# Products of the low-rank remainders with B, two tiles at a time in 64 rows of the array each

## What is computed

```python
x = x + L0(x)   # per head: causal convolution over the 512 positions with a filter K, plus x * D, then a mask by length
x = x + L1(x)   # per sequence b:
    result   = x[b] @ base_weight.T + base_bias          # 32 x 512 by 512 x 512
    h        = x[b] @ lora_A[adapter_ids[b]].T           # rank 16
    lora_out = h @ lora_B[adapter_ids[b]].T              # 16 -> 512
    return result + lora_out
```

## Time and profile before

| | us |
|---|---|
| median of 3 runs (lowest, highest) | 211.22 (211.07, 211.51) |
| the profiled execution | 210.73 |
| its span, first to last instruction | 208.8 |
| PE busy | 190.5 |
| DVE busy | 167.6 |
| ACT busy | 121.8 |
| POOL busy | 89.7 |

### The profile page before, as it was taken

One profiled execution on the slowest core, in us unless ns is written; L12 is line 12 of the kernel. 1 busy time (PEld: TensorE's weight loads), 2 busy tenths in 40 slices (PEclk: granted clock), 3 DMA queues, 4 the chain that ended last, 5 costly groups with the idle time before them and its releaser, 6 DMA issues.

```text
span 208.8 us, 4393 instructions
## 1 busy us (share of the span) xinstructions
PE 190.5 (91%) x1063; PEld 166.3 (80%) x1063; DVE 167.6 (80%) x366; ACT 121.8 (58%) x356; POOL 89.7 (43%) x144
## 2 busy tenths in 40 slices
PE   0049899999999999899999999999999999999993
PEld 0037899999999899788888888888888888888883
DVE  3985698789699976877999978788888878888662
ACT  2798865343636445337767656657566665756530
POOL 4850000001545778085563645546454464544500
PEclk9999999999999999999999999999999999999999
DMA  5984999999999999984877767657676677665334
GB/s 150 365 334 110 359 406 409 410 413 407 409 412 408 408 407 420 347 256 116 262 235 241 223 202 234 208 201 223 210 226 204 220 222 203 232 191 180 101 100 154
DMA packets 21521, 56.47 MB, mean 270 GB/s; under 512 B 3266, under 2 KB 3970, under 8 KB 21250
## 3 DMA queue, kind: packets, MB, share of 16 engines
q1 hardware_dynamic: 18146, 47.68, 62.3%
q0 software_dynamic: 2560, 8.39, 14.0%
q10 hardware_dynamic: 800, 0.23, 0.5%
HBM read 45.64 MB, written 10.65 MB: 270 GB/s over the span
## 4 chain that ended last, share of the span: by engine, by line
PE 82%; DMA 9%; DVE 5%; POOL 1%; issue 1%; SPq 0%; ACT 0%; DVEq 0%; ACTq 0%
PE z_ps L923 25%; PE y_ps L962 20%; PE k_ps L962 20%; DMA strip<-k_pad 7%; PE z_ps L950 7%; PE y_ps L989 2%; PE y_ps L988 2%; PE k_ps L989 2%; PE k_ps L988 2%; DMA par<-params 1%; DMA k_pad<-k_sb 1%; PE y_ps L1011 1%; PE k_ps L1011 1%; PE y_ps L972 1%; PE k_ps L904 1%
## 5 line engine op out<-in xcount | busy, mean ns | idle before, releaser
L923 PE MATMUL z_ps<-xp,strip 128*128 128x512 f32 (+3 forms) x384 | 63.6, 326 | 0.7 <-DMA strip<-k_pad 0.7
L923 PEld LDWEIGHTS z_ps<-xp,strip 128*128 128x128 f32 x384 | 59.3, 196 | 5.0 <-DMA strip<-k_pad 1.2
L410 POOL DMA_INDIRECT b_hl<-b_tab,b_idx x32 | 38.0, 1186 | 15.6 <-issue 9.0
L405 POOL CAST ag<-a_hl 128x128 fp32r x64 | 23.0, 361 | 40.7 <-PE z_ps L950 26.6
L962 PE MATMUL y_ps<-w_hi,xp 128*128 128x512 f32 x120 | 39.5, 390 | 0.0
L962 PE MATMUL k_ps<-w_hi,xp 128*128 128x512 f32 x120 | 39.5, 390 | 0.0
L543 ACT ACTIVATE ag<-a_hl 128x64 fp32r x128 | 25.6, 248 | 20.5 <-issue 20.3
L455 ACT ACTIVATE xp<-z_all 128x512 fp32r<-128x512 f32 x32 | 20.0, 629 | 21.4 <-PE z_ps L923 19.9
L736 DVE TENSOR_TENSOR xp<-z_all,xp 128x512 fp32r<-128x512 f32 x32 | 26.3, 823 | 5.3 <-ACT xp L455 5.2
L962 PEld LDWEIGHTS y_ps<-w_hi,xp 128*128 128x128 f32 x120 | 22.5, 188 | 4.3
L962 PEld LDWEIGHTS k_ps<-w_hi,xp 128*128 128x128 f32 x120 | 22.5, 188 | 4.3
(11 more groups left out here) (137 smaller groups left out, 237.9 us busy)
## 6 DMA issues: line engine op xcount, KB each, us to landing
strip<-k_pad SPq DMA_DIRECT2D x31, 512.0 KB, 7.8
z_all<-x_conv SPq DMA_DIRECT2D x16, 512.0 KB, 8.3
x_t<-x_tile SPq DMA_DIRECT2D x32, 256.0 KB
out<-a_raw SPq DMA_DIRECT2D x31, 256.0 KB
a_raw<-a_t SPq DMA_DIRECT2D x2, 512.0 KB, 7.6
x_t<-b_rows SPq DMA_DIRECT2D x2, 512.0 KB, 8.7
w_sb<-w_t SPq DMA_DIRECT2D x2, 512.0 KB, 9.9
b_tab<-b_hl SPq DMA_DIRECT2D x1, 1024.0 KB, 10.0
```

Source lines behind the costliest of these rows:

```text
L405: last = g.tensor_copy(ag[:, s, :, :, q, :].rearrange("p c e r -> p e c r"), src)
L410: g.indirect_dma_start(out=b_hl[:, t % BS, :].bitcast(F32), out_offset=None, in_=b_tab, in_offset=bass.IndirectOffsetOnAxis(ap=b_idx[:, t: ...
L923: last = nc.tensor.matmul(z_ps[:, h % ZS, m * P:L], strip[:, h % SS, m * P:(m + 1) * P, t], xp[:, h % XS, 0:LC - m, e, :], start=(n == 0), ...
```

## The change

The remainder of h no longer has zeros beside it. Tiles are paired (0 with 1, 2 with 3, up to 28 with 29). The even tile's h_lo lies in partitions 0 to 63 of a buffer, the odd tile's in 64 to 127 of the same buffer. For odd tiles the index table exchanges the halves of B, so that the high part of B lies in partitions 64 to 127 (`b_idx`, `table`). `tile_b` issues the h_hi product for each tile, and after that of the odd tile the two h_lo products of the pair, each over 64 rows, into two banks. A new semaphore `hhi_used` tells ACT that the h_hi product is done. `y_done` of both tiles comes after the odd tile, so DVE evicts both in the even step (`evict`), and none in the odd one. Tile 30 keeps a product over 128 rows, as does tile 31 in its halves; POOL zeroes the other half of their `h_lo` late (`lo_zeroed`), and no longer at the start.

```diff
+        def lo_half(t, s):
+
+            last = isinstance(t, int) and t == NT - 1
+            o = s % 2 * BR
+            return slice(o, o + BR), (s // 2 + last) % TS
...
-            link(g.memset(h_lo[BR:P, :, :].bitcast(F32), 0.0))
...
-            pool.wait_ge(idx_ready, 1)
+            pool.wait_ge(idx_ready, 2)
...
+            pool.wait_ge(gathered, NT)
+            pool.wait_ge(y_done, NT - 4)
+            g.memset(h_lo[BR:P, 1, :].bitcast(F32), 0.0).then_inc(lo_zeroed, 1)
+            pool.wait_ge(lo_zeroed, 1)
+            pool.wait_ge(y_done, NT - 2)
+            g.memset(h_lo[0:BR, 0, :].bitcast(F32), 0.0).then_inc(lo_zeroed, 1)
...
             def h_rounded(t, b, first):
                 act.wait_ge(hm_done, t + 1)
                 if not first:
-                    act.wait_ge(y_done, t + (1 - TS))
+                    act.wait_ge(hhi_used, t + (1 - TS))
...
-                V.tensor_scalar(b_idx[:, :], ids[:, NB:NB + NT], float(R), row_c, ALU.mult,
-                                ALU.add).then_inc(idx_ready, 1)
+                for o in range(2):
+                    V.tensor_scalar(b_idx[:, o::2], ids[:, NB + o:NB + NT:2], float(R), tab[:, NL + 2 + o:NL + 3 + o],
+                                    ALU.mult, ALU.add).then_inc(idx_ready, 1)
...
-            def h_remainder(t, b):
+            def h_remainder(t, s):
+
+                b, (rows, pair) = s % TS, lo_half(t, s)
                 dve.wait_ge(hhi_done, 2 * t + 2)
-                V.tensor_tensor(h_lo[0:BR, b, :], h_m[:, b, :], h_hi[0:BR, b, :].bitcast(F32),
+                V.tensor_tensor(h_lo[rows, pair, :], h_m[:, b, :], h_hi[0:BR, b, :].bitcast(F32),
                                 ALU.subtract).then_inc(hlo_done, 1)
+
+            def evict(i, s, lap, ago):
+
+                dve.wait_ge(y_done, i + (1 - ago))
+                if not isinstance(i, int) or i - ago >= OS:
+                    dve.wait_ge(stored[(s - ago) % OS], 16 * (lap + (s - ago) // OS))
+                V.tensor_tensor(o_sb[:, (s - ago) % OS, :], y_bank(s - ago), bias_sb[:, :], ALU.add).then_inc(o_done, 1)
...
+                elif known and i == NT - 1:
+                    evict(i, s, lap, 1)
+                elif s % 2 == 0 and there(i - 1):
+                    evict(i, s, lap, 2)
+                    evict(i, s, lap, 1)
...
-                nc.tensor.matmul(y_bank(s), h_hi[:, b, :], b_hl[:, s % BS, :], start=False, stop=False)
-                nc.tensor.matmul(y_bank(s), h_lo[:, b, :], b_hl[:, s % BS, :],
-                                 start=False, stop=True).then_inc(y_done, 1)
+                nc.tensor.matmul(y_bank(s), h_hi[:, b, :], b_hl[:, s % BS, :],
+                                 start=False, stop=False).then_inc(hhi_used, 1)
+                if isinstance(t, int) and t == NT - 2:
+                    pe.wait_ge(lo_zeroed, 1)
+                    nc.tensor.matmul(y_bank(s), h_lo[:, lo_half(t, s)[1], :], b_hl[:, s % BS, :],
+                                     start=False, stop=True).then_inc(y_done, 1)
+                elif s % 2:
+                    for q in (s - 1, s):
+                        rows, pair = lo_half(q, q)
+                        nc.tensor.matmul(y_bank(q), h_lo[rows, pair, :], b_hl[rows, q % BS, :],
+                                         start=False, stop=True).then_inc(y_done, 1)
...
+    table[:, NL + 3] = AD * R * (1 - np.arange(P) // BR) + np.arange(P) % R
```

More of the change, by code:

```diff
@@ L105, in build @@
         par = sb("par", [P, 7, NH])
-        tab = sb("tab", [P, NL + 3])
+        tab = sb("tab", [P, NL + 4])
         dt = sb("dt", [P, NH])
@@ L211, in build @@
         base_done, y_done, o_done = sem("base_done"), sem("y_done"), sem("o_done")
+        hhi_used, lo_zeroed = sem("hhi_used"), sem("lo_zeroed")
+        def lo_half(t, s):
+            last = isinstance(t, int) and t == NT - 1
+            o = s % 2 * BR
+            return slice(o, o + BR), (s // 2 + last) % TS
         def in_chunks(a):
@@ L715, in adapter_ids @@
                 dve.wait_ge(ids_in, 16)
-                row_c = tab[:, NL + 2:NL + 3]
                 link(V.tensor_copy(id_f[:, 1, :], ids[:, :]))
@@ L817, in step @@
                     h_masked(i + 1, (s + 1) % TS)
[L818 to L833, removed]
-                                        ALU.add).then_inc(o_done, 1)
+                if known and i == 2:
+                    dve.wait_ge(tab_lo_stored, 16)
+                    dve.wait_ge(bias_in, 16)
+                if known and i == NT:
+                    dve.wait_ge(stored[OS - 1], 16 * (NT // OS - 1))
+                    for n in range(2):
+                        cols = slice(n * L // 2, (n + 1) * L // 2)
+                        dve.wait_ge(y_done, NT + n)
+                        V.tensor_tensor(o_sb[:, OS - 1, cols], y_bank(YS - 1 + n)[:, 0:L // 2], bias_sb[:, cols],
+                                        ALU.add).then_inc(o_done, 1)
+                elif known and i == NT - 1:
[3 more added lines that the diff above has]
+                    evict(i, s, lap, 1)
                 if there(i + 4):
@@ L841, in step @@
                 if there(i + 1):
-                    h_remainder(i + 1, (s + 1) % TS)
+                    h_remainder(i + 1, s + 1)
             def part_of_x1(t, h0, h1, done):
@@ L1018, in last_b @@
                 pe.wait_ge(hlo_done, NT)
+                pe.wait_ge(lo_zeroed, 2)
                 nc.tensor.matmul(y, h_hi[:, b, :], b_hl[:, BS - 1, cols], start=False, stop=False)
-                nc.tensor.matmul(y, h_lo[:, b, :], b_hl[:, BS - 1, cols], start=False, stop=True).then_inc(y_done, 1)
+                nc.tensor.matmul(y, h_lo[:, lo_half(NT - 1, NT - 1)[1], :], b_hl[:, BS - 1, cols], start=False, stop=True).then_inc(y_done, 1)
             for t in range(NT - OS, NT - 2):
@@ L1050 @@
                        np.broadcast_to(g["L0_cond_log_dt"][None, :], (P, NH))], axis=1)
-    table = np.zeros((P, NL + 3), np.float32)
+    table = np.zeros((P, NL + 4), np.float32)
     table[:, 0:NL] = np.concatenate([NC * np.arange(NA), np.arange(NC)])
```

## The result

The kernel after takes 225.44 us (median of 4, 224.06 to 226.81), the kernel before, timed beside it, 211.14 (210.75 to 211.51). The ratio is 1.068 with a 95% interval of 1.0656 to 1.0705: slower. The sign was forecast, the size was not: 214.9 us, with a range to 218.3. The profiled execution took 224.98 us with a span of 222.9, from its first to its last instruction; before it was 210.73 and 208.8.

A forecast was written before the change was run, and what follows sets the result against it. The prediction took PE's stream of matmuls to bound the tile stage. The profiled 210.73 us plus 3.7 for shape changes, with 0 for the other engines, gave 214.4, and 0.49 to the median made 214.9; range 209.0 to 218.3.

The forecast's parts named there:

- a landing between the two: On SP, the x load was taken to land between 3.6 and 2.1 us after issue, costing 0.
- The ring: Through SP and DVE, even eviction to store, x load, landing and next eviction: 7.9 us per pair with landing 3.6.
- +0.245 us per pair: On PE, changing between 128-row and 64-row products was to cost this much more per pair, 3.7 us over 15 pairs.
- The offset b: On PE, the start of a pair's second 64-row product behind the first, taken as 0.09 us.
- The tail: At the end, late memsets, DVE's two evictions and last h remainder: level with PE, at most 0.1 us shows.
- hidden by about 1 us: On DVE, an even and an odd step together take 6.4 us against PE's 7.34 to 7.6 per pair: cost 0.
- The gathers: On POOL, B's gather for even tiles, released one tile later, lands in 3.7 us, 11 us ahead of use: cost 0.
- 1: On PE, switching shape is free and the two products lie side by side: 207.7 us, chance 0.17.
- 2: On PE, the change of shape costs its drain but hides its weight loads: 210.2 us, chance 0.12.
- 3: On PE, the two 64-row products run one behind the other, 0.23 us apart: 217.0 us, chance 0.21.
- Rival 4: On SP and DVE, the x load comes late, deciding from a 3.4 us landing on: 219.6 us, chance 0.04.
- Against it: Evidence against a late x load: DVE has no x_t wait from 91 to 201 us, and DMA engines are less loaded.

The follow-up runs named there:

- before_ahead7: The control: the kernel before with only the x load one tile further ahead (7 steps in place of 6); 210.79 us, ratio 0.9994 to 1.0023.
- ahead7: The kernel after with one constant changed, so that SP issues each x load one store earlier; 214.49 us.
- before_64: The kernel before with each tile's h_lo product over only the 64 nonzero rows, nothing beside it; 224.44 us.
- full_rows_ahead7: The kernel after with its h_lo products over all 128 rows and each x load issued one store earlier; 212.80 us.
- same_rows: The kernel after with x loads one tile further ahead and both 64-row products in rows 0 to 63, so not side by side; 218.24 us.
- quarter_both: The kernel after with stores of a quarter of the columns and B's gathers of 32 of 128 rows; 214.36 us.
- half_load: The kernel after with x loads (from tile 4 on) of half the columns, 128 KB; 217.05 us.

## Why the prediction was wrong

**The step that failed** is the one on SP: "so I take a landing between the two and a cost of 0". The ring itself was laid out rightly: 1.67 us from eviction to load, the landing, 2.6 back to the eviction, 4.27 in all where the runs show 4.4; and also that it decides from a landing of 3.4 us on (3.2 against the pair of 7.56). In before a landing between the two rows, 3.6 and 2.1, is right: the control has 2.7. In after the load in the ring takes 3.86, longer than either. The landing was judged by the mean traffic of the stage, 213 GB/s against 405. But the change puts two evictions into one step and lets the gathers of two tiles go within 4 us of a pair's end, so that stores, x loads and gathers come in pairs. The load in the ring, issued at 151.90, flies with the gather of 150.40, the stores of 151.15 and 152.53 and the x load of 153.63. Mean traffic says nothing of a burst that the change itself makes. What the ring costs is 10.95 us (after against ahead7); the prediction gave it a chance of 4% and 8.4 us. Even that rival would have come out at 219.6: against before, the pairs took 9.5 us more in the trace and the last one another 4.3.

**PE.** Forecast +0.245 us per pair, 3.7 in all; measured +0.155, 0.86 in place of 0.705. The terms but one stood: 0.32 to the first 64-row load, 0.43 from there to the next full one (0.11 of exposed load and 0.32), and another 0.11 behind that. The offset b between the two was taken as 0.09 from products of other shapes; it is 0.004. The rows give 15 x 0.155 = 2.3 us, the spans 2.5, the times 1.7. The Trainium skill's "TensorE: Matmul & The Clock Gate", Part 3, with its 4 ns, holds here: the records have 3 to 4 ns. The rule of the Trainium skill's "TensorEngine Tiling (Array Packing)", Key Properties, that a change of mode drains the array, agrees as far as the trace can tell: each change cost 0.09 and exposed a load of 0.11, in before_64 0.39 per trip. The prediction named both and worked with neither for b.

**What it also cost to be late in the ring.** The tail was put at 0.1 us; it is 4.1 over ahead7's, since the last x load is late, PE asks for tile 31's h right behind tile 30's, and from the end of that wait of 1.93 us the clock is at its lower level for 3.4 us. No rival named that.

**DVE.** "hidden by about 1 us" held as long as the load is early: no wait of PE in ahead7's stage. Yet full_rows_ahead7, whose PE work is that of before, is 1.6 us longer by its times and 0.75 by its spans. Its pairs take 7.39 us against 7.35, 0.7 in all. The 0.05 lie in the starts of the first products of a tile (0.238, 0.235 and 0.232 apart where before has 0.233, 0.230 and 0.227); why is open. In the profiled execution PE also waits 0.36 for ACT at the stage's start. The rest of the 1.6 lies outside the span.

**POOL.** The gathers were judged by whether they land in time for PE, 11 us ahead. They do. That they take the DMA engines while the x load flies wasn't asked, and it is the larger part of the cause: quartering them saves 6.9 us, quartering the stores 4.5.

**Rivals.** 1, 2 and 3 are out: switching isn't free (before_64), its loads aren't hidden, the products do lie side by side (same_rows). Rival 4 was the case, with what it named as its sign: DVE waits for x_t and PE waits for h_lo. "Against it" stood that DVE has no such wait before; but before, the even tile's store went a step earlier, so that absence told nothing of after.

## To carry to other kernels

When a step is moved later on one engine, follow every queue that it releases around to itself and write the circle down as a sum; where its long end lies above the bound, as 7.9 over 7.6 here, its length deserves more care than any other term. One load of distance more (one line) took it out here. Judge a landing by what the change issues at the same moment, not by mean traffic. And weigh row packing by trips: here one trip at 512 columns cost 0.39 us and two products side by side saved 0.235, so by an estimate it takes two such pairs per trip to win anything.

## What the runs showed of the hardware

- Two 64-row fp32r products in different halves of the array start 4 ns apart; in the same rows the second is 0.34 us behind (same_rows). One trip from 128-row products to 64-row ones and back costs 0.39 us (before_64).
- A 256 KB load took 2.7 us beside single stores and gathers (before_ahead7). In their burst the load in the ring took 3.9 (after), 2.9 with both cut to a quarter (quarter_both), and 3.1 at half its own size (half_load).
- After PE stood still 1.93 us at the end of after, the granted clock was 0.5 from 210.1 to 213.5 us. Products of 512 columns came 0.43 us apart there, and 0.227 behind it.
